# Two-layer attention and mixture-of-experts kernel: the queries' inverse root moves from GpSimd to VectorE, the weight fold is spread over three steps, and the expert beats are dealt out anew

## The reference, cut to what matters

```python
q = (h @ Wq_c @ Wq_up)...                                  # 16 heads of 128
q = rmsnorm(apply_partial_rope(q, cos, sin), q_norm_w)     # x * rsqrt(mean(x*x) + eps) * w
c_out = attend(q @ ck, valid, sink, ck)                    # 16 block keys
sw_out = attend(50*tanh(q @ k_sw / 50), window of 64, sink, v_sw)
inter = einsum('btgf,gfi->btgi', c_out + sw_out, Wg); out = inter @ Wo
# experts: 32 of them, top 6 of each token, relu(x @ w1 + b1) @ w2 + b2, weighted, plus 2 shared ones
```

## Time and profile before

| | us |
|---|---|
| median of 3 runs (lowest, highest) | 595.01 (593.98, 600.37) |
| the profiled execution's own time | 597.21 |
| its span, first to last instruction | 595.4 |
| PE / DVE / ACT / POOL busy in the span | 522.0 / 334.4 / 312.5 / 328.9 |

### The profile page before, as it was taken

One profiled execution on the slowest core, in us unless ns is written; L12 is line 12 of the kernel. 1 busy time (PEld: TensorE's weight loads), 2 busy tenths in 40 slices (PEclk: granted clock), 3 DMA queues, 4 the chain that ended last, 5 costly groups with the idle time before them and its releaser, 6 DMA issues.

```text
span 595.4 us, 9656 instructions
## 1 busy us (share of the span) xinstructions
PE 522.0 (88%) x2951; PEld 397.9 (67%) x2951; DVE 334.4 (56%) x884; ACT 312.5 (52%) x739; POOL 328.9 (55%) x235
## 2 busy tenths in 40 slices
PE   0998988799777899999999999999988898899981
PEld 0655776588566678778787777988856444465561
DVE  3389832314056282652935629343356898999643
ACT  1215126365464776757757577575632238666530
POOL 3000438868677586685866858854312024888860
PEclk9999999899797999999999999999999999999997
DMA  9940629887886986675675756866368102556667
GB/s 289 375 149 6 165 66 216 183 173 187 209 240 155 251 215 150 128 169 112 145 175 127 169 117 142 187 147 142 35 171 264 52 21 78 81 88 98 97 80 220
DMA packets 87281, 90.39 MB, mean 152 GB/s; under 512 B 26688, under 2 KB 75264, under 8 KB 86848
## 3 DMA queue, kind: packets, MB, share of 16 engines
q1 hardware_dynamic: 66608, 61.50, 36.1%
q0 software_dynamic: 19584, 27.24, 27.5%
q10 hardware_dynamic: 1040, 1.05, 0.5%
HBM read 65.32 MB, written 22.60 MB: 148 GB/s over the span
## 4 chain that ended last, share of the span: by engine, by line
PE 40%; DVE 18%; issue 15%; DMA 9%; ACT 9%; POOL 8%; SPq 0%; POOLq 0%; ACTq 0%; DVEq 0%
PE bank L559 8%; DMA expert_sums<-expert_weights,token_of_slot 7%; PE bank L896 6%; PE bank L904 3%; PE bank L905 3%; PE bank L551 2%; PE bank L523 2%; POOL tiles L1098 2%; PE bank L1804 2%; DVE sum_squares L686 2%; ACT normed L607 2%; POOL expert_sums L866 2%; POOL expert_weights L858 2%; POOL expert_sums L1105 2%; PE bank L491 2%
## 5 line engine op out<-in xcount | busy, mean ns | idle before, releaser
L866 POOL DMA_INDIRECT expert_sums<-expert_weights,token_of_slot x79 | 131.1, 1659 | 57.1 <-ACT expert_weights L928 39.4
L858 POOL DMA_INDIRECT expert_weights<-normed_x,token_of_slot x79 | 92.2, 1167 | 111.5 <-DVE token_of_slot L366 47.2
L896 PE MATMUL bank<-expert_weights 128*88 128x128 f32 x632 | 84.2, 276 | 1.3 <-ACT expert_weights L921 1.2
L896 PEld LDWEIGHTS bank<-expert_weights 128*88 128x88 f32 x632 | 74.6, 159 | 2.1 <-issue 2.1
L559 PE MATMUL bank<-out_weights,expert_weights 128*128 128x256 f32 x256 | 60.1, 380 | 1.4 <-ACT expert_weights L644 1.4
L928 ACT ACTIVATE expert_weights<-bank,chosen_bf 128x256 f32<-128x256 f32 x79 | 37.7, 478 | 36.4 <-issue 22.2
L904 PE MATMUL bank<-expert_weights 88*128 88x256 f32 x158 | 48.4, 388 | 6.9 <-ACT expert_weights L928 5.7
L1105 POOL DMA_INDIRECT expert_sums<-expert_weights,token_of_slot x23 | 46.3, 2011 | 14.5 <-issue 5.5
L559 PEld LDWEIGHTS bank<-out_weights,expert_weights 128*128 128x128 f32 x256 | 46.4, 190 | 8.2 <-ACT expert_weights L644 3.1
L719 DVE SCALAR_TENSOR_TENSOR expert_weights<-bank,blocks_valid 128x64 f32<-128x64 f32 x32 | 7.1, 221 | 75.6 <-ACT expert_weights L621 68.7
L905 PE MATMUL bank<-expert_weights 89*128 89x256 f32 x158 | 48.1, 385 | 0.0
(11 more groups left out here) (272 smaller groups left out, 1084.7 us busy)
## 6 DMA issues: line engine op xcount, KB each, us to landing
expert_weights<-experts_out SPq DMA_DIRECT2D x79, 192.8 KB
expert_weights<-experts_in SPq DMA_DIRECT2D x79, 176.0 KB
expert_weights<-L_ffn_wi SPq DMA_DIRECT2D x32, 128.0 KB
expert_weights<-w_comp SPq DMA_DIRECT2D x1, 2048.0 KB, 9.2
expert_weights<-fold_g SPq DMA_DIRECT2D x1, 2048.0 KB, 13.4
expert_sums<-zeros SPq DMA_DIRECT2D x2, 1024.0 KB, 17.9
expert_weights<-L_ffn_wo SPq DMA_DIRECT2D x16, 128.0 KB
normed<-expert_sums SPq DMA_DIRECT2D x2, 1024.0 KB, 5.6
```

Source lines behind the costliest of these rows:

```text
L858: nc.gpsimd.indirect_dma_start(xt0[g % 4], None, xn0, bass.IndirectOffsetOnAxis(ap=MAP[:, g:g + 1], axis=0)).then_inc(gathered[g % 4], 16)
L866: nc.gpsimd.indirect_dma_start(sums0[g % 2], bass.IndirectOffsetOnAxis(ap=MAP[:, g:g + 1], axis=0), yt0[g % 2], None, compute_op=ALU.add). ...
L896: ins = nc.tensor.matmul(ps[5][0:DHB, c * P:(c + 1) * P], w[:, k * DH + c * DHB:k * DH + (c + 1) * DHB], xT0[g % NXT][:, k * P:(k + 1) * P ...
```

## The change

Three edits. (1) `query_power` goes from POOL; `query_rms` on DVE forms mean + eps as before (still signalling `qss` there), then a seed by integer arithmetic on the bits and three Newton rounds, in place, on 128 x 16 numbers: ten instructions, nine of them followed by a wait of DVE for itself. (2) The fold's eight parts go to steps -1 (four), 0 (two) and 1 (two), in slots 1, 3, 4, 6 of step -1 and slots 4, 6 of steps 0 and 1. (3) Beats: four in step -1, six in step 0, eight in step 1, nine in steps 2 to 7 (two of them in slot 4, that is s = 0), seven in step 8. SyncE's loads of values move from beats 48 and 64 to 44 and 60.

```diff
-BEATS = {g: (1,) * 8 for g in range(FIRST_STEP, NT)}
-BEATS[NT] = (1,) * 7 + (0,)
+BEATS = {-1: (0, 1, 0, 1, 1, 0, 1, 0), 0: (1, 1, 0, 1, 1, 0, 1, 1), 1: (1,) * 8, **{g: (1, 1, 1, 1, 2, 1, 1, 1) for g in range(2, NT)},
+         NT: (1,) * 7 + (0,)}
+FOLDS = {(-1, 1): 0, (-1, 3): 1, (-1, 4): 2, (-1, 6): 3, (0, 4): 4, (0, 6): 5, (1, 4): 6, (1, 6): 7}
...
-                if g == 0:
-                    fold(pe, k)
+                if (g, k) in FOLDS:
+                    fold(pe, FOLDS[g, k])
...
-        def query_mean(st, t):
-            j = t % TPB
+        def query_rms(dve, st, t):
+
+            x = RR[:, t % TPB * H:(t % TPB + 1) * H]
+            y, a = RTMP[:, 0:H], RTMP[:, H:]
             st.wait()
-            nc.vector.tensor_scalar(RR[:, j * H:(j + 1) * H], SSQ[:, j * H:(j + 1) * H], 1.0 / D, RMS_EPS, ALU.mult, ALU.add).then_inc(qss, 1)
+            nc.vector.tensor_scalar(x, SSQ[:, t % TPB * H:(t % TPB + 1) * H], 1.0 / D, RMS_EPS, ALU.mult, ALU.add).then_inc(qss, 1)
+            dve.wait_ge(qss, t + 1)
+            st.link(nc.vector.tensor_scalar(y.bitcast(I32), x.bitcast(I32), -0.5, float(0x5f3759df), ALU.mult, ALU.add))
+            for i in range(3):
+                st.link(nc.vector.tensor_tensor(a, y, y, ALU.mult))
+                st.link(nc.vector.scalar_tensor_tensor(out=a, in0=a, scalar=-0.5, in1=x, op0=ALU.mult, op1=ALU.mult))
+                if i < 2:
+                    st.link(nc.vector.scalar_tensor_tensor(out=y, in0=a, scalar=1.5, in1=y, op0=ALU.add, op1=ALU.mult))
+            nc.vector.scalar_tensor_tensor(out=x, in0=a, scalar=1.5, in1=y, op0=ALU.add, op1=ALU.mult).then_inc(qpow, 1)
...
-                    if i == 48:
+                    if i == 44:
                         sp.wait_ge(pv_ps, NWIN)
-                    if 48 <= i < 49 + NWIN:
-                        load_values(sp, 2, i - 48)
-                    if i == 64:
+                    if 44 <= i < 45 + NWIN:
+                        load_values(sp, 2, i - 44)
+                    if i == 60:
                         sp.wait_ge(pv_ps, 2 * NWIN)
...
-                power_at = {beats(g, NG)[0]: g + 1 for g in range(FIRST_STEP, NT - 1)}
...
-                    if i in power_at:
-                        query_power(pool, power_at[i])
```

More of the change, by code:

```diff
@@ L179, in build @@
         SSQ = sb("sum_squares", 2 * H)
+        RTMP = sb("rms_steps", 2 * H)
         KW = sb("norm_columns", 4)
@@ L473, in load_values @@
                 sp.dma_start(vw[n:NWK, i, :], VA[lo2:lo2 + NWK - n, (b * TPB + 1) * D:(b * TPB + 2) * D]).then_inc(vw_ld[b % 2], 16)
[L475 to L479, removed]
         def up_queries(pe, t, j):
@@ L592, in attention_pe @@
                         turn_probs(pe, g - 2, s + 1)
-                if g == 0:
-                    fold(pe, NG + s)
+                if (g, NG + s) in FOLDS:
+                    fold(pe, FOLDS[g, NG + s])
                 for i in beats(g, NG + s):
@@ L662, in attention_act @@
                     probs_T(act, g - 2, 0)
-                if g == 0:
-                    take_folded(act, k)
+                if (g, k) in FOLDS:
+                    take_folded(act, FOLDS[g, k])
             for s in range(NSUB):
@@ L671, in attention_act @@
                         probs_T(act, g - 2, s + 1)
-                if g == 0:
-                    take_folded(act, NG + s)
+                if (g, NG + s) in FOLDS:
+                    take_folded(act, FOLDS[g, NG + s])
                 for i in beats(g, NG + s):
                     expert_act(act, i)
-        def query_mean(st, t):
-            j = t % TPB
+        def query_rms(dve, st, t):
+            x = RR[:, t % TPB * H:(t % TPB + 1) * H]
+            y, a = RTMP[:, 0:H], RTMP[:, H:]
             st.wait()
-            nc.vector.tensor_scalar(RR[:, j * H:(j + 1) * H], SSQ[:, j * H:(j + 1) * H], 1.0 / D, RMS_EPS, ALU.mult, ALU.add).then_inc(qss, 1)
+            nc.vector.tensor_scalar(x, SSQ[:, t % TPB * H:(t % TPB + 1) * H], 1.0 / D, RMS_EPS, ALU.mult, ALU.add).then_inc(qss, 1)
[7 more added lines that the diff above has]
+            nc.vector.scalar_tensor_tensor(out=x, in0=a, scalar=1.5, in1=y, op0=ALU.add, op1=ALU.mult).then_inc(qpow, 1)
         def query_squares(dve, st, t):
@@ L686, in query_squares @@
             st(nc.vector.reduce_sum(SSQ[:, t % 2 * H:(t % 2 + 1) * H], v3(SQ, H), AX))
-            query_mean(st, t)
+            query_rms(dve, st, t)
         def query_rotate(dve, t):
@@ L1529, in _ @@
                         sp.dma_start(BONES, a["table_by_head"]).then_inc(ld_w1, 16)
-                    if 64 <= i < 65 + NWIN:
-                        load_values(sp, 3, i - 64)
+                    if 60 <= i < 61 + NWIN:
+                        load_values(sp, 3, i - 60)
                 for i in range(2):
```

## The result

The kernel after takes 592.7 us (median of 20 runs, 589.9 to 599.3), the kernel before 596.1 (20 runs, 593.6 to 600.9). The ratio is 0.9937 with an interval of 0.9914 to 0.9961: 0.6% faster, where 2.6% (580 us) was forecast, and outside the range given (574 to 588). The profiled execution took 592.0 us, against 597.2.

What follows compares the result with a forecast made beforehand. PE's own list was taken to bound steps 3 to 6, POOL's pace the lightest early steps, DVE part of step 1. Gain 29.9 less 14.5 is 15.4 us: 595.0 to 579.6, say 580, range 574 to 588.

Steps and rivals of the forecast that it cites:

- the first three steps: Steps -1, 0 and 1: 17.8, 18.2 and 35.4 us, together 71.4 instead of 101.3, a gain of 29.9.
- POOL has 2.2 us of slack over the first ten beats: Steps -1 and 0, argued against a smaller early gain: even at PE's pace POOL keeps up, 35.9 against 32, without power.
- without the 2.29, about 1.2 of the 1.86, and the half clock: Step 1, first half: these waits and about 3 us of half clock go, so 20.4 us becomes 13.9.
- The prediction's own sign of being wrong: Wrong if step 1 stays near 40 us, the ten instructions exceed 3 us, or the clock dips in a later step.
- the early gain is smaller: Steps 0 and 1: adds still land late, beats 11 to 15 bunched; 9 us less gain, 588.6 us; chance 0.16.
- its waits stay: Step 2, first half: its 5 us of idle stays, so the added beat costs its full 1.96 us.
- what the new beats 44 and 60 hold up on SyncE's queue: Steps 4 and 6: the moved loads of values hold up no weight load; cost zero.
- The later steps: Steps 2 to 7: 11.8 us for six added beats plus 2.7 for longer waits, 14.5 us lost.
- The root's price: On DVE, ten instructions at 0.22 us: 2.2 us for each tile, bounds 1.8 and 3.7.
- the dear root: On DVE: root instructions cost more than taken; gain gone at 0.48 us each; 596 to 603 us, chance 0.06.
- the clock: Steps 2 to 6: waits of 1.5 us at the last `scores` lower the clock, 13 us lost; 592.6 us; chance 0.06.
- 29.9 - 14.5: Whole kernel: gain of steps -1 to 1 less loss of steps 2 to 7, 15.4 us.

Runs made afterwards that it cites:

- four outputs: The kernel after with four buffers for the experts' outputs instead of two, and layer 1's last expert loaded at the end: 578.6 us, ratio 0.9702.
- four outputs in both kernels: Adds the kernel before with the same four output buffers and late expert load, its beats, folds and power untouched: 588.8 us, against 578.6 for the kernel after.
- the root alone: The kernel before with only the root moved to DVE and no power on POOL, beats and folds untouched: 612.2 us, ratio 1.0277.
- the last two kernels: Kernel after with four output buffers, late bulk writes, root moved to the step's end before the queries' norm; doubled beat in slot 4: 574.5 us, slot 5: 569.5.

## Why the prediction was wrong, step by step

**The step that failed** is the one on the first three steps that ends in "POOL has 2.2 us of slack over the first ten beats" (the numbers beside it, 35.9 against 32, differ by 3.9), and with it "without the 2.29, about 1.2 of the 1.86, and the half clock". I counted the pace of POOL's queue, which was the right reading of step -1, and took the waits for line 928 as its result. They have two parts: POOL's lateness, and the 3.8 to 7.6 us (5.1 at the median) that an add takes to land, which with two buffers must fit between a tile and the second one after it, where PE at its pace takes 3.9 for two beats. Where one step meets the next, beats 12 to 15 and 21 to 23 follow each other by 1.9 to 2.5 us, and no slack of POOL's earlier helps them. Waits of 1.84, 3.36 and 4.64 stayed or grew, the last two with half clock, and steps 0 to 2 took 10.0 us more than forecast. With four outputs they are 12.8 us shorter. Steps -1, 0 and 1 are then 18.0, 17.8 and 34.7, where 17.8, 18.2 and 35.4 were forecast, and the time is 578.6, where 580 was: the working of PE's, DVE's and POOL's parts held, for a kernel whose landings cost nothing. The prediction's own sign of being wrong, step 1 near 40 us, came (39.6).

**The rival "the early gain is smaller"** named this mechanism, the adds that land late, and its sign of bunched beats 11 to 15. It had the size wrong: 9 us in steps 0 and 1, where 7.2 were lost, and nothing in step 2, of which I had said that its waits stay. The first of them grew from 2.17 to 4.64 beside the bulk writes, whose beat numbers were not changed and which therefore met the start of step 2. The prediction looked at what the new beats 44 and 60 hold up on SyncE's queue, and not at transfers that stayed at their beat.

**Step 2** was 37.4 in the forecast and 40.2; on four outputs 35.6. The ninth beat cost its full price there, as forecast: with four outputs in both kernels the step goes from 33.4 to 35.6, 2.2 us for a beat of 1.96. What was off is "by waits that stay": the 2.17 among them is a wait for a landing too, which grew with two outputs and goes with four.

**The later steps** were right: 39.8 for 40.0, 35.1 for 35.2. The root's price was right (2.2 for each tile). Its effect was 0.1 on the last `scores`' wait and not 0.54, because the doubled beat delays ACT, and DVE with it, by more than I counted as cover. It cost nothing there, and 3.9 a step without that beat, where the forecast had 2.2: the rest is half clock. Of the two rivals priced for it, the dear root did not occur; the clock did where the cover was missing (a wait of 2.59), and not at 1.08.

**Sum.** Forecast 29.9 - 14.5 = 15.4. By the steps of the two traces: 6.4 + 16.0 + 0.1 - 5.3 - 9.2 - 1.9 = 6.1 gained, less 1.6 for the later start, and 0.7 gained behind step 7: the spans differ by 5.2 (595.4 and 590.2). The medians differ by 3.4.

## What to carry to other kernels

When work is bunched so that an engine keeps busy, follow every ring of buffers that the bunched items go through to the landing of its transfer, not only to its issue: with two buffers and 5.6 us to a landing, two items together take at least 5.6, whatever slack the queue has. A transfer tied to a loop index moves in time when the loop is dealt out anew, so look at those that the diff doesn't touch as well. A small serial chain is free where its engine waits for another anyway; find that place from the trace of the new order, since it is the neighbour's work that makes it.

## What the runs showed of the hardware

An add of 128 rows of 1 KB, scattered into memory, took 3.8 us to land at the least, 5.1 at the median and 7.6 beside bulk writes of 1152 KB (after, 84 to 250 us); one of 6.9 stands far from them, at 201.3. With two output buffers it was this time, and not the 1.58 of its issue, that held the beats up.

POOL's issue of such a transfer was stretched while DVE multiplied the queries by the root: an add 2.49 instead of 1.58, a gather 2.20 instead of 0.99, and the gather 0.99 again with that multiply cut short. The Trainium skill ("SBUF — State Buffer", the section on the two separate sides) warns that DVE, by holding the port pair that it shares with GpSimd, can keep the latter from writing the descriptors of its transfers. It names DVE operations in a fast mode for that, and those with two inputs only against a GpSimd operation that reads SBUF; here a multiply of two fp32 arrays in SBUF did it. The gather and the add take their row numbers from a table in SBUF (`token_of_slot`), so the second case may be what is seen; no run tells the two apart.

A wait of 2.6 us once a step was followed by half clock in steps that are otherwise dense (granted 0.96 over the step, the root alone), one of 1.08 at the same place by none (1.00, after). The length of the wait didn't settle it: in step 1 of the last two kernels, with the same instructions there, a wait of 1.62 was followed by half clock and one of 1.64 by none:

```profile
148.10:151.60 3.50, 3.50 (x16) 3.23 (x15) 2.40 (x11) 1.90 (x5) 2.81 (x3) 0.52 0.68 103
```
```profile
150.00:154.00 4.00, 3.96 (x32) 3.80 (x33) 2.94 (x11) 2.54 (x7) 3.12 (x3) 1.00 0.83 185
```

(The clock is the third number from the right.) The first window is of the root at the end with the doubled beat in slot 4, the second of the same with it in slot 5.
